# Sixteen-batch decoder, one core: the steps of neighbouring layers put in alternation instead of one layer after the other

## The reference, cut to what matters

```python
x = layernorm(x + L0_attn(x))                 # multi-query attention, 8 heads of 128, causal
x = layernorm(x + L0_xattn(x, ctx))           # 16 heads of 8, causal
x = layernorm(x + L0_ffn(x))                  # mixture of 8 experts, top 2, SiLU
x = layernorm(x + L1_attn(x))                 # 16 heads of 8, windows of 64 with a bias by position
x = layernorm(x + L1_xattn(x, ctx))           # 16 heads of 8
x = layernorm(x + L1_ffn(x))                  # mixture of 8 experts, linear
x = layernorm(x + L2_attn(x))                 # 16 heads of 8, rotary, causal
x = layernorm(x + L2_xattn(x, ctx, mask))     # 16 heads of 64, scores clipped
x = layernorm(x + L2_ffn(x))                  # quantised: needs maxima over the whole tensor
x = layernorm(x + L3_attn(x))                 # 16 heads of 8, rotary, causal
x = layernorm(x + L3_xattn(ctx, x, mask))     # 16 heads of 64, 256 keys
x = layernorm(x + L3_ffn(x))                  # SiLU
```

## Time and profile before

| | us |
|---|---|
| median of 3 runs | 1938.68 (1937.98 to 1938.98) |
| span of the profiled execution, first to last instruction | 1932.0 |
| median less span (what lies around the instructions) | 6.7 |
| PE busy in that span | 1736.0 (90%) |
| DVE busy | 1378.8 (71%) |
| ACT busy | 1340.0 (69%) |
| POOL busy | 837.3 (43%) |

### The profile page before, as it was taken

The page is one execution under the profiler, slowest core; times in us unless marked ns, Lnnn a source line. Parts: engine busy times, 40 slices in busy tenths (PEclk is TensorE's granted clock), DMA queues, the critical chain, the costliest instruction groups (busy, mean ns, idle before and its releaser), DMA issues. The chain is left out here.

```text
span 1932.0 us, 40599 instructions
## 1 busy us (share of the span) xinstructions
PE 1736.0 (90%) x13884; PEld 1294.5 (67%) x13945; DVE 1378.8 (71%) x3901; ACT 1340.0 (69%) x5411; POOL 837.3 (43%) x998
## 2 busy tenths in 40 slices
PE   6999999999888898789999999615889999999998
PEld 6886558889655565246688888404556777777777
DVE  4667886777888898988844444595998656566665
ACT  3447986565899996159977777442988666666666
POOL 2235770000566785147733333121776433333345
PEclk9999999999988999789999999866999999999999
DMA  7000000000000000000000000200000000000000
GB/s 285 1 1 1 2 2 2 1 2 2 2 1 2 2 2 2 1 1 2 2 2 1 2 1 2 117 0 1 1 2 2 1 1 1 1 1 1 1 1 23
DMA packets 5819, 22.98 MB, mean 12 GB/s; under 512 B 624, under 2 KB 2672, under 8 KB 4720
## 3 DMA queue, kind: packets, MB, share of 16 engines
q1 hardware_dynamic: 5616, 20.39, 2.7%
HBM read 19.34 MB, written 1.05 MB: 11 GB/s over the span
## 5 line engine op out<-in xcount | busy, mean ns | idle before, releaser
L1394 POOL TENSOR_TENSOR a_probs<-a_probs,a_rinv 128x512 f32<-128x512 f32 x352 | 365.7, 1040 | 318.0 <-DVE a_rinv L1238 314.5
L1047 ACT ACTIVATE a_probs<-bank,a_negmax 128x128 f32<-128x128 f32 x896 | 324.8, 434 | 12.9 <-DVE a_negmax L1218 12.8
L1394 POOL TENSOR_TENSOR c_probs<-c_probs,c_rinv 128x512 f32<-128x512 f32 x192 | 200.1, 1042 | 163.5 <-DVE c_rinv L1238 160.4
L889 PEld LDWEIGHTS bank<-const,a_probs 128*128 128x128 f32 x1408 | 159.0, 144 | 134.0 <-issue 110.2
L1047 ACT ACTIVATION_READ_ACCUMULATOR a_probs<-bank,a_negmax 128x1 f32 x896 | 237.5, 275 | 0.0
L889 PE MATMUL bank<-const,a_probs 128*128 128x128 f32 x1408 | 231.4, 288 | 1.9 <-DVE a_probs_t L1245 0.9
L1422 POOL TENSOR_TENSOR a_rstd<-a_ve,neg_half 128x1 f32<-128x1 f32 x128 | 70.2, 549 | 341.1 <-DVE a_ve L1296 340.9
L1218 DVE TENSOR_REDUCE a_negmax<-bank 128x4 f32<-128x512 f32 x224 | 152.0, 680 | 20.5 <-PE bank L857 16.6
L857 PE MATMUL bank<-a_kz,a_qk 32*128 32x512 f32 x512 | 148.1, 655 | 2.2 <-DVE a_probs L1216 1.6
L1238 DVE RECIPROCAL a_rinv<-a_rsum 128x4 f32<-128x4 f32 x352 | 59.7, 170 | 113.7 <-ACT a_probs L1043 107.8
L1245 DVE COPY a_probs_t<-bank 128x512 f32<-128x512 f32 x176 | 120.5, 684 | 25.8 <-PE bank L889 24.7
(11 more groups left out here) (254 smaller groups left out, 4418.9 us busy)
## 6 DMA issues: line engine op xcount, KB each, us to landing
w_L_ffn<-in_L_ffn SPq DMA_DIRECT2D x1, 3184.0 KB, 20.4
w_L_xattn<-in_L_xattn SPq DMA_DIRECT2D x1, 2112.0 KB, 29.5
w_L_xattn<-in_L_xattn SPq DMA_DIRECT2D x1, 2050.0 KB, 9.9
w_L_attn<-in_L_attn SPq DMA_DIRECT2D x1, 1345.5 KB, 23.1
w_L_attn<-in_L_attn SPq DMA_DIRECT2D x1, 1157.0 KB, 6.7
ctx_t<-in_ctxT SPq DMA_DIRECT2D x1, 1024.0 KB, 13.0
w_L_attn<-in_L_attn SPq DMA_DIRECT2D x2, 512.0 KB, 14.7
ctx<-in_ctx SPq DMA_DIRECT2D x1, 1024.0 KB, 13.3
```

Source lines behind the costliest of these rows:

```text
L889: mm = pe.transpose(bank[:, j * S:(j + 1) * S], Pb[:, n % PB, j * S:(j + 1) * S], ident)
L1047: op = act.activation(p, bank_of("scores", n)[:, j * width:(j + 1) * width], ACT.Exp, bias=negmax[:, n % PB, j:j + 1], accum_out=rsum[:, n ...
L1394: pool.tensor_tensor(p, p, along(rinv[:, n % PB, 0:heads], 512 // heads), ALU.mult).then_inc(sems["norm_done"], 1)
```

## The change

`Plan` gets a weave: a list of (start, leading layer, following layer, lag). Step b of the leader is placed at start + b, step b of the follower at start + b + lag + 0.5, and all steps are sorted by that. A pair may begin before the pair ahead of it has ended; then three layers alternate. In loop A the pairs are L0_attn with L0_xattn (lag 6), L0_ffn with L1_attn (lag 2), L1_xattn with L1_ffn (lag 6) and L2_attn with L2_xattn (lag 4), 16 places apart. In loop C L3_attn and L3_xattn alternate (lag 4), and L3_ffn follows alone. The rest of the diff keeps the buffers right when the kinds mix: rings counted by family of kinds, the last user of a slot of a ring looked up instead of computed, and a buffer of its own for `odd_sum`. One table entry moves: the moe router is issued 18 slots ahead instead of 26. No instruction of the computation is added or removed.

```diff
-    "moe": [("router", 26, "dve"), ("gateT", 6, "act"), ("biases", 2, "dve")],
+    "moe": [("router", 18, "dve"), ("gateT", 6, "act"), ("biases", 2, "dve")],
...
+WEAVE_A = [(0, 0, 1, 6), (16, 2, 3, 2), (32, 4, 5, 6), (48, 6, 7, 4)]
+WEAVE_C = [(0, 0, 1, 4), (21, 2, None, 0)]
+
+
+def woven(weave):
+
+    when = {}
+    for start, lead, follow, lag in weave:
+        for b in range(G):
+            when[lead, b] = start + b
+            if follow is not None:
+                when[follow, b] = start + b + lag + 0.5
+    return sorted(when, key=when.get)
...
-        self.steps = [(L, b) for L in range(len(layers)) for b in range(G)]
+        self.steps = woven(weave)
...
+        family = H8 if self.kind(s) in H8 else (self.kind(s),)
+        return sum(self.kind(t) in family for t in range(s)) % n
+
+    def out_ring(self, s, n):
+
         return sum(self.kind(t) in SOFTMAX for t in range(s)) % n
+
+    def last_in_slot(self, s, n):
+
+        b = self.steps[s][1]
+        same = [t for t in range(s) if self.steps[t][1] % n == b % n]
+        return same[-1] if same else None
...
-                odd_sum = HS[:, 0, :, :]
+                odd_sum = sb(tag + "odd_sum", [P, 2, D], scope=scope)
...
-                if s >= R_RING:
-                    wait_once(eng, sems["x_ready"], s - R_RING + 1)
+                before = plan.last_in_slot(s, R_RING)
+                if before is not None:
+                    wait_once(eng, sems["x_ready"], before + 1)
```

More of the change, by code:

```diff
@@ L213, in ring, with slot_before @@
     def ring(self, s, n):
+        family = H8 if self.kind(s) in H8 else (self.kind(s),)
+        return sum(self.kind(t) in family for t in range(s)) % n
+    def out_ring(self, s, n):
         return sum(self.kind(t) in SOFTMAX for t in range(s)) % n
+    def last_in_slot(self, s, n):
+        b = self.steps[s][1]
+        same = [t for t in range(s) if self.steps[t][1] % n == b % n]
+        return same[-1] if same else None
+    def slot_before(self, n, size):
+        kind = self.kind(self.units[n][0])
+        same = [m for m in range(n - size, -1, -size) if self.kind(self.units[m][0]) == kind]
+        return same[0] if same else None
     def layer(self, s):
@@ L675, in state_t_ready @@
                 elif not last_loop:
-                    wait_once(eng, first_in["xT", int(s >= FIRST)], 16)
+                    wait_once(eng, first_in["xT", int(plan.steps[s][1] >= FIRST)], 16)
             def state_ready(eng, s):
@@ L682, in state_ready @@
                 elif not last_loop:
[L683 removed]
+                    wait_once(eng, first_in["x", int(plan.steps[s][1] >= FIRST)], 16)
             def sum_free(eng, s):
[L687 to L688 removed]
+                before = plan.last_in_slot(s, R_RING)
+                if before is not None:
+                    wait_once(eng, sems["x_ready"], before + 1)
             def attended(s, kind):
@@ L737, in hidden_free @@
             def hidden_free(eng, n):
-                if n >= PB and plan.unit(n - PB)[2] == plan.unit(n)[2]:
-                    wait_once(eng, sems["second_ready"], plan.count("second", n - PB))
+                before = plan.slot_before(n, PB)
+                if before is not None:
+                    wait_once(eng, sems["second_ready"], plan.count("second", before))
             with nc.Block() as block:
@@ L747, in _ @@
                         for b in range(G):
-                            sp.wait_ge(sems["x_ready"], (len(plan.layers) - 1) * G + b + 1)
+                            sp.wait_ge(sems["x_ready"], plan.steps.index((len(plan.layers) - 1, b)) + 1)
                             sp.dma_start(out[b:b + 1].rearrange("a p d -> p (a d)"), X[:, b, :]).then_inc(sems["x_out"], 16)
@@ L951, in output @@
                         for c in range(chunks):
-                            mm = pe.matmul(bank[:, 0:D], OT[:, plan.ring(s, 2), c, :], W(s, "Wo")[:, c * D:(c + 1) * D], start=c == 0, stop=c == chunks - 1)
+                            mm = pe.matmul(bank[:, 0:D], OT[:, plan.out_ring(s, 2), c, :], W(s, "Wo")[:, c * D:(c + 1) * D], start=c == 0, stop=c == chunks - 1)
                         mm.then_inc(sems["proj_ready"], 1)
@@ L1053, in front @@
                             act.wait_ge(sems["scores_ready"], plan.count("scores", n))
-                            if n >= 3 and plan.unit(n - 3)[2] == "moe":
-                                wait_once(act, sems["gate_done"], plan.count("gate", n - 3))
+                            before = plan.slot_before(n, 3)
+                            if before is not None:
+                                wait_once(act, sems["gate_done"], plan.count("gate", before))
                             for j in range(2):
@@ L1405, in mask @@
                         if b >= MASK_RING:
-                            wait_once(pool, sems["moved"], plan.count("moved", plan.last[s - MASK_RING]))
+                            wait_once(pool, sems["moved"], plan.count("moved", plan.last[plan.steps.index((plan.steps[s][0], b - MASK_RING))]))
                         if plan.kind(s) == "h64m":
```

16 lines of the change are left out of this document (8 added, 8 removed).

## The result

The changed kernel takes **2219.3 us** (median of 4 runs, 2217.85 to 2223.92) where the kernel before took 1938.33 beside it (4 runs, 1937.93 to 1938.98): ratio 1.146, 95% interval 1.144 to 1.147, 281 us slower. I had forecast 1874 us. Neither the number nor the sign came out, and even the rival that ended on this side (1966) is 253 us short.

A forecast was written before the change was run, and what follows sets the result against it. PE was busy nine tenths of the span, but the busiest engine changed from layer to layer. Mixture gains of 64.8 us took the profiled 1932.0 to about 1867; with 6.7 for the median, 1874 us, range 1841 to 1915.

The forecast's parts named there:

- Which engine is the busiest in which layer: Per layer: PE alone in L0_attn, L2_xattn, L3_xattn; ACT, PE close behind, in h8 kinds; DVE in L1_ffn.
- Table loads: On ACT: 12 more at 1.283 us, 15.4 us; costing nothing if behind PE, 15 if all on the path.
- "Taken": Each mixture's forecast time: floor (largest engine's sum of work) plus about a third of the distance back; gains 64.8 us.
- The heaviest term: L0_ffn with L1_attn in loop A: 21.89 us a pair falls to 19.2, floor 18.3; gain 26.9 us over 10.
- Rival 3: Shared score banks: 47 claims each stall PE for a 1.95 us slot, 92 us on top, 1966 us; chance 0.08.
- Rival 2: Woven pairs: PE waits after four slots full of DVE and ACT work; gain only 27, 1912 us; chance 0.17.
- the sign that I had named for rival 3: In the changed profile: idle PE before the scores of the follower's first units, released by DVE; no size given.
- The sign for rival 2: In the changed profile: idle PE before transposes, released by POOL or ACT; no size given.
- theory L: From the experiments: weaving heaps DVE's and ACT's work into full slots, so removing one PE wait brings the next.

The follow-up runs named there:

- e10: e8 with the transpose of L0_ffn's gates issued 4 slots ahead instead of 6, rank and choice kept in place: 1977.8 us, ratio 1.020.
- e3: Changed kernel with only loop C woven, plus a fourth bank for L3_xattn's scores: 1966.7 us, ratio 1.015 to the kernel before.
- e8: Changed kernel with only L0_ffn and L1_attn woven, and the moe router 19 slots ahead instead of 18: 1978.5 us, ratio 1.021.
- e15: e10 with the maxima, exponentials and normalisations of L1_attn one slot later: 1990.8 us, ratio 1.028.
- e6: e3 with L3_attn's value projection issued 7 slots ahead instead of 6: 1941.3 us, ratio 1.0017.
- e5: Changed kernel, all weaves kept, with a fourth score bank for L0_attn and L3_xattn: 2169.3 us, ratio 1.119.

## Why the prediction was wrong

- **Which engine is the busiest in which layer**: right, and it still holds; DVE and POOL took the same time to 3 us, ACT its table loads.
- **Table loads**: right in size (12 more at 1.28; the earlier trace rows has 27 of the 32 loads before) and too small to matter: the 12 are 15.4 us in all, against 281. What part of them lies on the path was not measured apart.
- **"Taken", the floor plus a third of the distance back. This is the step that failed.** It assumed that streams in order have enough room between them that sums of work set the time, with a small surcharge for lumps. Measured, each of the six mixtures of the table lies above its old time, not between floor and old time: 274 us lost where these six were to gain 56. That layers of one kind run within 0.8 us of their busiest engine was the wrong neighbour to size this by. A layer of one kind repeats one pattern, and its leads (3 to 6 slots for the scores), its ring of banks and the place of each small copy go with that pattern; in the mixture they meet those of another kind, such as a ring of three beside a ring of four. That one bank and one lead more give back 68 of 71 us in loop C shows it there. For the other mixtures, where 56 more came back with all entries changed, it is in part argued.
- **The heaviest term, L0_ffn with L1_attn, -26.9.** I named the right place: DVE with four masked maxima, router, rank and choice in four slots, ahead of the copies that free PE's banks. I priced it at 0.9 us a pair (19.2 for 18.3). It is 7.4 above the floor in the change (25.7) and 6.5 in the best version (24.8). Slack elsewhere in the pair did not pay for one full place: in e10 PE stops 3.7 us for a 0.34 us instruction.
- **Rival 3, bank waits.** Its mechanism is shown for loop C (e3: 43 us for one more bank). Its price was a slot of DVE's work, at most 1.95 us; the stop measured 3.58, nearly two slots, because DVE was late already, and the half clock behind it was nowhere in the sum. I also counted score banks alone, while the router, the transpose of the gates and the value products (L821, L824, L963) stop PE as often.
- **Rival 2, lumps not carried.** Borne out in kind by e8 and e10, where the stop moved with each repair; e15, where it shrank by 1.3 us when one maximum was moved, fits. In size it had the wrong sign: it let the pair keep a third of the gain.
- **The rule for such changes.** The Trainium skill ("Perfetto Trace Analysis", Optimization Strategy) says that a kernel whose busiest engine changes from regime to regime may gain by interleaving them, beside work within each. This kernel is such a case by the earlier trace rows, and none of the four pairs woven alone, nor all five together, came out faster: the runs do not bear that "may" out here, with 0.2% more at best (e6, not to be told from none) and 14.6% for all of them.
- **The clock was left out of the sum.** The rows had it: L1_ffn, with PE idle a quarter of the time, was granted 0.75, and L1_attn 0.88. I read these as facts about layers that do not need PE. They were a sign of what idle time on PE costs anywhere, and it is nearly half of the loss (134 of 286).
- **What would show it.** Idle PE released by DVE does stand before scores, the sign that I had named for rival 3 (L886, 30.4 us), but before those of the leader L3_attn and not of the follower; before the followers' scores of loop A it is ACT that releases PE (L886 and L889 with ACT's L1079). The sign for rival 2, idle PE before transposes released by POOL or ACT, is nearly absent in the change (1.1 us for POOL at L921); it came with e15. I had given rivals 2 and 3 together 0.25, and the range ended at 1915, just past rival 2.

What stays open: the remaining 4 us a pair of L1_xattn with L1_ffn, and 15 us a step of the triple mixture. The timelines show what releases each stop, but I took none of those away; that they are theory L's is argued, not shown. That other leads for L1_attn with L0_ffn would do better than e10 is possible too. Other lags between leader and follower, or a plan without the triple mixture, were not tried.

## What to carry to other kernels

Before you interleave two tuned streams, do not add up busy times; list for each in-order engine what stands in one slot of the mixture ahead of the small instruction that another engine waits for, and price a stop by that whole queue, plus the clock it costs TensorE afterwards. An engine at 90% with a whole clock has little to win (5% at the floors here) and much to lose. If you weave, put kinds that share banks on one ring of the same length, and refit the leads for one pair at a time, since most of each loss shows up in the pair woven alone (71, 55, 62 and 9 us here); e5 warns that a repair in one mixture can still cost time in another.

## What the runs showed of the hardware

The long stops of PE that are shown here cost about twice their length, since the clock falls with them. After the 3.58 us stop before 1912.56 the matmul rows read 1.12 for 0.66 and 2.08 for 1.13; the granted clock was 0.50 from 1911.4 to 1921.6, and the rows are normal again from 1924.60. With 8.5 us of matmuls at half speed, about 4.2 us are lost beside the 3.58 (an estimate from this row). After the 3.73 us stop of e10, L910 takes 1.91 for the 1.06 that the same eight matmuls take at other times. Over the kernel, 152 us more idle time went with 134 us more busy time for the same matmuls.

Shorter stops did it too. In the kernel before, the stops of 1.6 us in L1_attn and of 1.0 to 2.2 us in L1_ffn lie in the two stretches that were granted 0.88 and 0.75:

```profile
534.14 0.49 PE L952 MATMUL bank<-w_L_attn,a_ot 128*128 128x128 f32 x2 [1.62 <-ACT a_ot L1088]
...
793.89 0.30 PE L964 MATMUL bank<-const,state 128*128 128x128 f32 x1 [2.17 <-DVE state L1301]
```

The other eight stretches, at 1.00, hold no stop of 0.9 us or more but one of 1.47 in L3_attn.

The Trainium skill ("Perfetto Trace Analysis", Identifying the Most-Contended Engine) holds the busy share of matmuls a bad measure of how near TensorE is to its peak, and names the weight loads' busy share beside the share of peak flops. On the first the trace agrees: the matmul share fell from 90% to 84%, by 6%, while the same work took so much longer that the work done per us fell by 13%. On the second it does not: the share of the weight loads fell by 6% too (67% to 63%), since their busy time rose by 102 us (1294.5 to 1396.6) for the same loads.
